# Attention in 64-row tiles, with the rotation of queries and keys moved from VectorE to GpSimd

## The reference

```python
x = x + attn0(layernorm(x)); x = x + moe0(layernorm(x))
x = x + attn1(layernorm(x)); x = x + moe1(layernorm(x))
# attn0: 16 heads of 16, RMS norm of q and k per head
q, k, v = split(y @ w_qkv)
q, k = rmsnorm(q) * gamma_q, rmsnorm(k) * gamma_k
q, k = (t * cos + rotate_half(t) * sin for t in (q, k))
p = softmax(where(causal, q @ k.T / 4, -1e30))
out = concat_heads(p @ v) @ w_out
# attn1: 16 query heads share one key head and one value head, no RMS norm,
# rotary tables with a scale (xPos), and a bias on the output
```

## Time and profile before

| | |
|---|---|
| median of 3 runs | 1419.74 us (1417.56 to 1423.05) |
| the profiled execution, its time and its span | 1433.71 us, 1431.9 us |
| mean granted TensorE clock | 0.848 |
| busy over the span: PE, PEld, DVE, ACT, POOL | 71%, 58%, 52%, 30%, 38% |

### The profile page before, as it was taken

One profiled execution on the slowest core, in us unless ns is written; L12 is line 12 of the kernel. 1 busy time (PEld: TensorE's weight loads), 2 busy tenths in 40 slices (PEclk: granted clock), 3 DMA queues, 4 the chain that ended last, 5 costly groups with the idle time before them and its releaser, 6 DMA issues. The chain is left out here.

```text
span 1431.9 us, 22633 instructions
## 1 busy us (share of the span) xinstructions
PE 1010.7 (71%) x6358; PEld 827.7 (58%) x6358; DVE 740.1 (52%) x1996; ACT 426.4 (30%) x1045; POOL 541.5 (38%) x740
## 2 busy tenths in 40 slices
PE   0289999998687894489998878660003999999910
PEld 0177777777554683377777756430003888887810
DVE  1677877774452355666555625620001555554567
ACT  1144444443110341134444322000001444444400
POOL 0022222221235363233333312366663566565610
PEclk9989999998679897599999975785556999999965
DMA  9000000000512453000000009133333556555467
GB/s 308 24 1 2 1 0 0 0 0 1 198 39 94 131 152 120 29 1 1 1 0 0 0 2 373 64 115 119 119 116 123 167 173 178 165 173 153 131 247 282
DMA packets 73707, 136.17 MB, mean 95 GB/s; under 512 B 14590, under 2 KB 52365, under 8 KB 71568
## 3 DMA queue, kind: packets, MB, share of 16 engines
q1 hardware_dynamic: 52016, 84.63, 18.5%
q0 software_dynamic: 17568, 46.71, 9.2%
q10 hardware_dynamic: 4032, 3.75, 0.8%
HBM read 78.66 MB, written 62.39 MB: 99 GB/s over the span
## 5 line engine op out<-in xcount | busy, mean ns | idle before, releaser
L1643 POOL DMA_INDIRECT parts<-e_y,e_dest x206 | 202.6, 984 | 176.4 <-issue 112.1
L996 POOL TENSOR_SCALAR_AFFINE_SELECT a_probs<-a_probs 128x256 f32<-128x256 f32 x256 | 110.0, 454 | 305.0 <-ACT a_probs L700 304.0
L1538 PE MATMUL e_ps_u<-wres,e_xT 128*128 x824 | 215.5, 385 | 0.1
L1251 POOL DMA_INDIRECT rows<-d_rows,d_place_at x160 | 153.6, 960 | 117.5 <-DMA rows<-d_rows,d_place_at 59.8
L1608 DVE TENSOR_TENSOR e_hid<-e_act_out,e_ps_u 128x128 f32<-128x128 f32 x206 | 59.3, 288 | 242.6 <-ACT e_act_out L1579 165.6
L1530 PE MATMUL e_ps_x<-ident,e_xg 128*128 128x128 f32 x412 | 80.4, 278 | 146.4 <-DMA e_xg<-rows 146.4
L1538 PEld LDWEIGHTS e_ps_u<-wres,e_xT 128*128 128x128 f32 x824 | 158.2, 193 | 23.1 <-issue 1.6
L1530 PEld LDWEIGHTS e_ps_x<-ident,e_xg 128*128 128x128 f32 x412 | 58.7, 144 | 169.0 <-DMA e_xg<-rows 148.1
L847 DVE TENSOR_REDUCE a_block_max<-a_ring 128x6 f32<-128x768 f32 x128 | 119.3, 950 | 22.2 <-PE a_ring L523 21.9
L1574 ACT ACTIVATE e_xT<-e_ps_x 128x256 f32<-128x256 f32 x206 | 78.9, 383 | 172.5 <-PE e_ps_x L1530 171.9
L700 ACT ACTIVATE a_probs<-a_ring 128x768 f32<-128x768 f32 x128 | 103.7, 810 | 82.0 <-PE a_ring L551 80.4
(11 more groups left out here) (220 smaller groups left out, 2124.3 us busy)
## 6 DMA issues: line engine op xcount, KB each, us to landing
e_xg<-rows SPq DMA_DIRECT2D x159, 160.0 KB
e_yk<-parts SPq DMA_DIRECT2D x16, 1024.0 KB, 6.6
wres<-in_experts SPq DMA_DIRECT2D x4, 3072.0 KB
e_xg<-rows SPq DMA_DIRECT2D x47, 144.0 KB
wres<-in_experts SPq DMA_DIRECT2D x4, 1536.0 KB
rows<-setup_empty SPq DMA_DIRECT2D x32, 160.0 KB
e_yk<-parts SPq DMA_DIRECT2D x16, 256.0 KB, 2.9
parts<-e_y,e_dest POOLq DMA_INDIRECT x206
```

Source lines behind the costliest of these rows:

```text
L996: last = nc.gpsimd.affine_select(out=diagonal[:, :, a], in_=diagonal[:, :, a], compare_op=ALU.is_ge, fill=0.0, base=0, pattern=[[0, 2], [1 ...
L1251: nc.gpsimd.indirect_dma_start(out=rows[:, :], out_offset=bass.IndirectOffsetOnAxis(ap=place_at[:, t, k:k + 1], axis=0), in_=X[:, t], in_o ...
L1538: last = nc.tensor.matmul(ps_u[b % 2][:, 0:2 * P], xT[b % 2][:, c * P:(c + 1) * P], wres[:, ds(e, 1), 2 * c * P:2 * (c + 1) * P].rearrange ...
L1643: nc.gpsimd.indirect_dma_start(out=parts[:, :], out_offset=bass.IndirectOffsetOnAxis(ap=dest[b % NY][:], axis=0), in_=y[b % NY][:], in_off ...
```

## The change

Scores of a pair are made by two matmuls over 64 rows each, side by side in the array, and `kT` loses its zeros; `sel_head` and `maxT` are laid out twice, in both halves of the rows, and one product of 384 columns takes the place of two. `attend` takes four heads in one step (its `i` counts quads) and `probs` has four buffers. `rotate` moves to GpSimd with the same four operations, after cut 1 (tile 0) and after cut 3 (tile 1). The orders are rewritten, and the loops over sequences are unrolled.

```diff
-NPB = 3
+NPB = 4
-PE_ORDER = ("t0 t1 t2 a0 t3 a1 t4 a2 t5 a3 t6 a4 h0 t7 a5 g0 g1 a6 g2 g3 a7 g4 g5 g6 g7".split(),
-            "t0 t1 t2 a0 t3 a1 t4 g0 a2 t5 g1 a3 t6 g2 a4 h0 t7 a5 g3 a6 g4 a7 g5".split())
-ACT_ORDER = ("e0 e1 e2 e3 e4 e5 o0 s0 e6 s1 c0 e7 c1 c3 c5 c7 o1".split(),
+PE_ORDER = ("t0 t1 t2 t3 a0 t4 t5 a1 t6 t7 h0 a2 a3 g0 g1 g2 g3 g4 g5 g6 g7".split(),
+            "t0 t1 t2 t3 a0 t4 g0 t5 g1 a1 t6 g2 t7 h0 a2 g3 g4 a3 g5".split())
+ACT_ORDER = ("e0 e1 e2 e3 e4 e5 o0 e6 e7 o1 s0 s1 c0 c1 c2 c3 c5 c7".split(),
              "e0 e1 e2 s0 e3 s1 e4 c0 e5 c1 o0 e6 e7 c3 c4 o1".split())
-DVE_ORDER = ("l0 n0 l1 c2 c4 c6".split(), "l0 l1 c2 n0 c5".split())
+ROTATE_AFTER = (1, 3)
+DVE_ORDER = ("n0 l0 l1 c4 c6".split(), "l0 l1 c2 n0 c5".split())
...
-                copy(kT[p][0:STK, at:at + count, 0, cols], src[0:STK])
-                last = copy(kT[p][STK:P, at:at + count, 1, cols], src[STK:P])
+                last = copy(kT[p][:, at:at + count, cols], src)
...
             def scores(s, p, j):
-                for hh in range(2):
-                    out = ring[:, 2 * (j % 2) + hh]
-                    nc.tensor.matmul(out[:, 0:P], qT[p][:, j, 0:P], keys(p, j, hh)[:, 0:P],
+                banks = [ring[:, 2 * (j % 2) + hh] for hh in range(2)]
+                for hh, out in enumerate(banks):
+                    nc.tensor.matmul(out[:, 0:P], qT[p][half_rows(hh), j, 0:P], keys(p, j, hh)[:, 0:P],
                                      start=True, stop=False, skip_group_check=True)
...
             def transpose_maxima(s):
-                for t in range(TB):
+                for i, t in enumerate((0, 1, 1)):
...
             def shifted_scores(s, p, j):
-                    nc.tensor.matmul(out[:, 0:N], sel_head[:, 2 * j + hh], maxT[:, 0:N],
-                                     start=False, stop=False, skip_group_check=True)
-                    last = nc.tensor.matmul(out[:, N:TRI], sel_head[:, 2 * j + hh], maxT[:, P:N],
-                                            start=False, stop=True, skip_group_check=True)
+                for hh, out in enumerate(banks):
+                    last = nc.tensor.matmul(out[:, 0:TRI], sel_head[half_rows(hh), 2 * j + hh],
+                                            maxT[half_rows(hh), 0:TRI], start=False, stop=True,
+                                            skip_group_check=True)
...
-            def attend(s, p, j):
-                pe.wait_ge(cut_done, PAIRS * s + j + 1)
+            def attend(s, p, i):
+                pe.wait_ge(cut_done, PAIRS * s + 2 * i + 2)
...
+                for row, vh, pr in quad:
                     nc.tensor.matmul(ps_av[row:row + HV, col:col + N], v[p][:, 0, vh], pr[:, 0:N],
                                      start=col == 0, stop=False, skip_group_check=True)
+                for row, vh, pr in quad:
                     last = nc.tensor.matmul(ps_av[row:row + HV, col + P:col + N], v[p][:, 1, vh], pr[:, N:TRI],
                                             start=False, stop=True, skip_group_check=True)
...
             def exponentials(s, j):
                 if j >= NPB:
-                    act.wait_ge(av_ps, PAIRS * s + j - NPB + 1)
+                    act.wait_ge(av_ps, QUADS * s + (j - NPB) // 2 + 1)
             def outputs(s, half):
-                act.wait_ge(av_ps, PAIRS * s + (half + 1) * PAIRS // 2)
+                act.wait_ge(av_ps, QUADS * s + (half + 1) * QUADS // 2)
...
-            nc.vector.tensor_copy(maxT[:], zero[:].to_broadcast([P, N]))
+            nc.vector.tensor_copy(max_stack[:].rearrange("p t c h s -> p (t c h s)"),
+                                  zero[:].to_broadcast([P, TB * P]))
             for i in range(2):
-                for hh, rows in ((0, slice(STK, P)), (1, slice(0, STK))):
-                    for c in range(kT[i].shape[1]):
-                        nc.vector.tensor_copy(kT[i][rows, c, hh], zero[rows].to_broadcast([STK, N]))
...
         def _(pool):
+            def rotate(s, t):
+                half = HD // 2
+                if t == 0:
+                    pool.wait_ge(qn_done, s + 1)
+                else:
+                    turn_done(pool, s - 1, "qk1")
+                passed(pool, waited_pool)
+                for (src, which), (dst, _) in zip(rot_parts(qn, t), rot_parts(rot_c, t)):
+                    last = nc.gpsimd.tensor_tensor(dst, src, table(tab_c, t, which, src.shape[2]), ALU.mult)
+                pool_rot.inc(last)
+                for (src, which), (dst, _) in zip(rot_parts(qn, t), rot_parts(rot_s, t)):
+                    for a, b in ((0, half), (half, 0)):
+                        last = nc.gpsimd.tensor_tensor(dst[:, :, :, a:a + half], src[:, :, :, b:b + half],
+                                                       table(tab_s, t, which, src.shape[2], a, a + half), ALU.mult)
+                pool_rot.inc(last)
+                wait(pool, stack_hi, TB * s)
+                pool_rot.wait(pool)
+                nc.gpsimd.tensor_tensor(rotated[:, t], rot_c[:, t], rot_s[:, t], ALU.add).then_inc(rot_done, 1)
+
             def sequence(s, p, before, after):
...
                 for j in range(PAIRS):
                     cut(s, j)
+                    if after and j == 0:
+                        pool_rot.start(s + 1)
+                    if after and j in ROTATE_AFTER:
+                        rotate(s + 1, ROTATE_AFTER.index(j))
...
-            with pool.Fori(0, (B - 2) // 2) as r:
-                for k in range(2):
-                    sequence(2 * r + 1 + k, (1 + k) % 2, True, True)
+            for s in range(1, B - 1):
+                sequence(s, s % 2, True, True)
```

More of the change, by code:

```diff
@@ L22 @@
 STK = 4 * HD
+QUADS = PAIRS // 2
 TRI = N + P
@@ L320, in attention @@
         qT = [sb(f"qT{i}", [P, PAIRS, N], F32R) for i in range(2)]
-        kT = [sb(f"kT{i}", [P, PAIRS if multi else 1, 2, N], F32R) for i in range(2)]
+        kT = [sb(f"kT{i}", [P, PAIRS if multi else 1, N], F32R) for i in range(2)]
         zero = sb("zero", [P, 1])
@@ L553, in shifted_scores @@
                 last.then_inc(st_ps, 1)
-            def attend(s, p, j):
-                pe.wait_ge(cut_done, PAIRS * s + j + 1)
-                if j == 0 and multi:
+            def attend(s, p, i):
+                pe.wait_ge(cut_done, PAIRS * s + 2 * i + 2)
+                if i == 0 and multi:
                     pe.wait_ge(v_done, s + 1)
-                elif j == 0:
+                elif i == 0:
                     pe.wait_ge(qn_done, s + 1)
                     turn_done(pe, s - 1, "qk1")
-                if j % (PAIRS // 2) == 0:
-                    wait(pe, av_out, 2 * s + 2 * j // PAIRS)
-                for hh in range(2):
-                    h = 2 * j + hh
-                    pr, vh, row, col = probs[:, j % NPB, hh], h if multi else 0, HV * (h % 4), N * (h // 4 % 2)
+                if i % 2 == 0:
+                    wait(pe, av_out, 2 * s + i // 2)
+                col = N * (i % 2)
+                quad = [(HV * n, 4 * i + n if multi else 0, probs[:, (2 * i + n // 2) % NPB, n % 2])
+                        for n in range(4)]
+                for row, vh, pr in quad:
@@ L746, in _ @@
             sequence(0, 0, False, True)
-            with act.Fori(0, (B - 2) // 2) as r:
-                for k in range(2):
-                    sequence(2 * r + 1 + k, (1 + k) % 2, True, True)
+            for s in range(1, B - 1):
+                sequence(s, s % 2, True, True)
             sequence(B - 1, (B - 1) % 2, True, False)
@@ L815, in norm_qk @@
                 ins.then_inc(t_out[bank["qk1"]] if t else qn_done, 1)
-            def rotate(s, t):
-                half = HD // 2
-                if t == 0:
-                    dve.wait_ge(qn_done, s + 1)
-                else:
-                    turn_done(dve, s - 1, "qk1")
-                for (src, which), (dst, _) in zip(rot_parts(qn, t), rot_parts(rot_c, t)):
-                    last = nc.vector.tensor_tensor(dst, src, table(tab_c, t, which, src.shape[2]), ALU.mult)
-                dve_rot.inc(last)
-                for (src, which), (dst, _) in zip(rot_parts(qn, t), rot_parts(rot_s, t)):
-                    for a, b in ((0, half), (half, 0)):
-                        last = nc.vector.tensor_tensor(dst[:, :, :, a:a + half], src[:, :, :, b:b + half],
-                                                       table(tab_s, t, which, src.shape[2], a, a + half), ALU.mult)
-                dve_rot.inc(last)
-                dve_rot.wait(dve)
-                wait(dve, stack_hi, TB * s)
-                nc.vector.tensor_tensor(rotated[:, t], rot_c[:, t], rot_s[:, t], ALU.add).then_inc(rot_done, 1)
             def stack_los(s, t):
@@ L899, in prepare @@
                 norm_qk(s, p, 1)
-                dve_rot.start(s)
-                for t in range(TB):
-                    rotate(s, t)
-                dve_rot.end()
             def sequence(s, p, before, after):
@@ L950, in _ @@
             sequence(0, 0, False, True)
```

(20 more changed lines are left out.)

46 lines of the change are left out of this document (26 added, 20 removed).

## The result

The changed kernel takes **1516.15 us** as median of four runs (1514.69 to 1517.46), the kernel before 1418.78 on the same chip. The ratio is 1.0678, with a 95% interval of 1.066 to 1.0695: +97 us where +60 was forecast, and 1 us above the upper bound of 1515. The profiled execution took 1517.46 us (span 1515.7), at a mean granted clock of 0.767 where the kernel before had 0.848. Four later executions (1710, 1710 and 2151 us of the kernel before, 1422 of x8) fell in a slower state of the chip and are counted in no ratio and no median.

A forecast was written before the change was run, and what follows sets the result against it. The prediction took TensorE (PE) to bound stage C, with GpSimd's queue the bound after the change. 57.4 + 13.3 + 5.6 - 12 - 4.7 = 59.6, some +60 us, gave a median of 1480 us, range 1448 to 1515.

The forecast's parts named there:

- the walk through GpSimd's queue: Layer 0 stage C: cuts, rotations, o1, stacking and groups follow one another to 29.05 us; +8.2 each, seven times +57.4.
- Rival 1: Contention: GpSimd's rotation stretched throughout by VectorE or its short runs; half gives 1507, all of it 1533; chance 0.12.
- rival 3: Faster kernel: each microsecond less per layer 0 rotation tile takes 14 x 1.65 = 23 us; chance 0.05.
- Rival 2: Row tiles don't overlap: stage A loses 1.6 us sixteen times and dips fall on it; 1506 to 1510; chance 0.08.
- I take nothing: Stage A: tiled steps and mode changes take about the 0.69 us a pair of now; bounds 0.9 won, 1.6 lost.
- The price of 0.14: PE's mode change: 0.14 us or more per round trip between score steps and attend in stage C.
- the step "Clock": PE's idle stretches in stage C lower the clock: 0.8 us per layer 0 sequence, +5.6; bounds 0 and 1.9.
- Layer 1: Stage C 19.2 against 17.98 us, wider maxima +0.2, clock 0.5: 1.9 per sequence, seven times +13.3.
- The small terms: Last sequences without rotation -6 us each, -12; preamble -4.7, with its slower rotation costing only +1.0.
- The list of signs in the forecast: What would show it wrong: early qn, rotation under 3 us, groups under 5, stage A more than 1 us shorter.

The follow-up runs named there:

- x8: The changed kernel with rotation on VectorE, mask in 64-row tiles, s0 and s1 ahead of o1 in layer 0, plus filler matmuls: 1411.59 us, ratio 0.9775.
- x1: The changed kernel with the rotation back on VectorE, all else as changed: 1431.9 us, ratio 0.9955 to the kernel before.
- x5: The changed kernel with the stacks and groups of layer 0 drawn ahead of o1 and a3: 1519.17 us, ratio 1.0534 to the kernel before.
- x4: The changed kernel with unused filler matmuls in PE's idle stretches of layer 0's stage C: 1527.63 us, ratio 1.063 to the kernel before.
- y1: The kernel before with stage A's scores in 64-row tiles, mask still on the full array: 1452.99 us, ratio 1.021.
- x7: The changed kernel with stage A again over all 128 rows, stage C still in tiles: 1519.18 us, ratio 1.0554 to the kernel before.
- x2: The kernel before with only the rotation moved to GpSimd, after cuts 1 and 3: 1530.96 us, ratio 1.0645.
- x9: x6 with stage A over all 128 rows as in x7: 1404.99 us, ratio 0.9768 to the kernel before.
- x6: x1 with the mask in 64-row tiles and, in layer 0, s0 and s1 ahead of o1: 1412.18 us, ratio 0.9796 to the kernel before.

## Why the prediction was too low

**Right.** The direction, and the walk through GpSimd's queue. Stage C of layer 0 was put at 29.05 and took 28.45; seven of them cost 54.3 where I had 57.4. Its links hold one by one: `qn` at 5.5 us (5.4), rotation 3.98 (4.0), last cut 17.9 (18.45), `s0` behind `o1` until 19.5 (20.0), then eight groups. x1 takes the rotation away from GpSimd, and 7.45 us per stage go; x5 changes only the order behind it, and 3 go. Rival 1, contention, fell: the rotation runs at 1.27 for 512 elements, the upper end of the uncontended rows. The Trainium skill (GPSIMD Engine Reference, Performance versus the Vector engine) puts two-input operations at about twice VectorE's time; 1.27 against VectorE's 0.69 to 0.81 agrees nearly. Its factor as an estimate, 4.8 us a tile, would have added 18 and not 15 to the forecast's sum, by rival 3's own rate (14 x 1.65 x 0.8).

Rival 2 fell in its premise: the two row tiles overlap (0.11 a step in stage C). But the 20 us and more that it would have brought came by another way. That 1516 lies so near the upper bound of 1515 is luck: the bound was worked out from rivals 1 and 2, and neither came true.

**Wrong: "I take nothing" for the mode changes of stage A.** The working said that 0.46 + 0.2 is about the 0.69 of now. The pair measured 0.86 at full clock and 1.45 at the low one, against 1.28 for the full array there (the second and third pair of a low stage of before):

```profile
222.14 0.44 PE L518 MATMUL a_ring<-a_kT,a_qT 128*128 128x128 f32 x1 [1.47 <-ACT a_kT L686]
...
222.92 0.31 PE L518 MATMUL a_ring<-a_kT,a_qT 128*128 128x128 f32 x1
...
224.20 0.31 PE L518 MATMUL a_ring<-a_kT,a_qT 128*128 128x128 f32 x1
```

The price of 0.14 came from one exchange between a pair and `attend` in stage C; rounded up to 0.2 it stood for the two changes in every pair, and 0.86 less the 0.46 of steps is 0.4. At full clock this hardly shows: VectorE's eight maxima hold the stage, and layer 1 went from 13.2 to 13.6. At the low clock PE holds it, and the five pairs that fall into it (268.39 to 278.88) cost 0.17 more each, some 0.9 us of the 4.2 by which a middle stage A grew. This is an estimate from the rows above.

**Wrong: the step "Clock", the largest miss.** I added 0.8 us per sequence of layer 0, bounds 0 and 1.9, for idle stretches in stage C. The sign was right and the cause, for most of it, was not. The size was misread too: 0.81 over 16.31 us means 6.3 us at 1.2 GHz, and not most of the stage. Fillers that end the long idle stretches leave the low clock in stage A at 11.2 us (x4); 64-row steps in an otherwise unchanged kernel bring it to 13.3 (y1); full-array steps behind a sparse stage C end it within 6.4 (x7). The stages A of layer 0 gave +31.1 instead of +5.6. Of the 4.2 us that a middle stage grew, 3.2 vanish with full-array scores (x7, 16.2 instead of 19.4), the 0.9 of mode changes among them; the last 1.0 is the low clock's 5.1 us there instead of 3.3, which the sparse stage C may have brought; x2 has 5.0 too.

**Layer 1, mis-sized.** +26.9 instead of +13.3. Its first stage A lies wholly at the low clock, 16.47 instead of 12.23 (+4.2); in x9, over the full array, it is 12.5. Stage C took 20.8 on the mean, where 19.9 was forecast with its clock and its wider maxima. The walk holds up to the last exponential, which ends at 777.84, 16.55 into the stage (forecast 16.6). Then the tail takes 4.1 where I had 2.6:

```profile
777.77 1.08 PE L575 MATMUL a_ps_av<-a_probs,a_v 128*32 128x256 f32 x8
778.62 0.65 PE L578 MATMUL a_ps_av<-a_probs,a_v 128*32 128x128 f32 x8
779.20 1.25 PE L505 MATMUL a_ps_t<-ident_r,a_stack 128*128 128x128 f32 x8
780.39 0.74 PE L575 MATMUL a_ps_av<-a_probs,a_v 128*32 128x256 f32 x8
```

`a2` and two groups stand ahead of `a3` at the low clock; I had counted `a3` alone at full clock.

**The small terms.** The last stage C of layer 0 is 12.41, not 11.4 (17.40 - 6), at a clock of 0.72; the preamble won 2.5, not 4.7. In x1, whose preamble has the rotation on VectorE, the first score comes 3.5 earlier still (73.5), so there the rotation cost 3.5 and not 1.0.

The list of signs in the forecast looked for a stage A that is *shorter* than expected, and for none that is longer. Layer 0's rows of a low stage should have raised that question: with 6.3 us at the low clock PE is busy for 16.18 of 16.31, against 13.68 of 14.41 without, so PE has no slack left there, and a later return of the clock lengthens the stage.

**Open.** The stages of each kernel are read from one execution, and how far the low clock's length varies from one to the next is not known. Why 64-row steps hold the granted clock down is not shown; no run here tells apart how many rows are in use, how many columns stream and how often the mode changes. The profile's busy time doesn't decide it either: it counts a matmul's whole latency, so it would hide short pauses of the array, as at a change of mode. All-tile stages scatter between 0 and 13.1 us, alternating ones lie between 8 and 13.7 but for one of 5.8. Filling helped all-tile stages (x6 to x8, 10.2 to 7.1) and not alternating ones (x4, 10.7 to 11.2), and that stays unexplained.
